# Expert stages of a macaron transformer block: answers copied out a quarter step sooner, last sends unpaced, and the second gated stage's end rearranged

## The reference

```python
x = L0_attn_x
x = x + 0.5 * _L0_ffn_ref(_layernorm(x), expert_sel, keys, values)        # 32 gated experts, top 4
x = x + _L0_attn_ref(_layernorm(x), Wq, ..., projection)                  # linear attention, 16 heads
x = x + 0.5 * _L0_ffn_ref(_layernorm(x), expert_sel, keys, values)        # the second gated stage
x = x + 0.5 * _L1_ffn_ref(_layernorm(x), Wg, W1, b1, W2, b2)              # experts, first time
x = x + _L1_attn_ref(_layernorm(x), P_q, P_k, P_v, P_o)                   # softmax diagonal, 16 heads
x = x + 0.5 * _L1_ffn_ref(_layernorm(x), Wg, W1, b1, W2, b2)              # experts, second time

def _L1_ffn_ref(x, Wg, W1, b1, W2, b2):    # 8 experts, 2 of them for each token
    gates = softmax(xt @ Wg); idx1, idx2 = best and second best expert of each token
    pos1, pos2 = position of the token among its expert's tokens, in order of choice
    xe[idx, pos] += xt * keep
    h = gelu(xe @ W1 + b1);  ye = h @ W2 + b2
    out = ye[idx1, pos1] * w1 + ye[idx2, pos2] * w2
```

## Time and profile before

| what | value |
|---|---|
| median of 3 runs | 1787.54 us (1783.36 to 1790.53) |
| the profiled execution | 1795.37 us, its span 1793.6 us |
| PE busy | 1441.7 us, 80% of the span |
| DVE busy | 1343.0 us, 75% |
| ACT busy | 1077.9 us, 60% |
| POOL busy | 858.8 us, 48% |
| granted PE clock, mean | 0.925 of full speed |

### The profile page before, as it was taken

How to read it: one execution, slowest core, us unless ns; L and a number is a source line. 1 busy time by engine, 2 the same in 40 slices (tenths; PEclk the granted TensorE clock), 3 DMA queues, 4 the chain that set the end, 5 groups by cost and what they waited for, 6 DMA issues and landing times. The chain is left out here.

```text
span 1793.6 us, 30589 instructions
## 1 busy us (share of the span) xinstructions
PE 1441.7 (80%) x8651; PEld 1048.8 (58%) x8653; DVE 1343.0 (75%) x3826; ACT 1077.9 (60%) x2260; POOL 858.8 (48%) x742
## 2 busy tenths in 40 slices
PE   5899988896999994998527888888888699679880
PEld 4677767654666653776415666566566466357660
DVE  7588887565667666776676999999999667757766
ACT  6677752364122325777437999999999522267770
POOL 6666642210034343565626666666666124636663
PEclk9899998898999996999859999999999899789995
DMA  5997001000001114222129930000000001122225
GB/s 106 142 176 115 1 1 25 1 1 24 16 30 43 30 33 93 55 67 60 41 85 183 179 59 1 1 1 1 1 1 1 1 16 34 42 59 59 59 57 143
DMA packets 182175, 91.71 MB, mean 51 GB/s; under 512 B 43829, under 2 KB 176902, under 8 KB 182048
## 3 DMA queue, kind: packets, MB, share of 16 engines
q1 hardware_dynamic: 167840, 71.19, 21.5%
q0 software_dynamic: 9984, 16.89, 2.9%
q10 hardware_dynamic: 4224, 2.10, 0.4%
HBM read 32.59 MB, written 61.18 MB: 52 GB/s over the span
## 5 line engine op out<-in xcount | busy, mean ns | idle before, releaser
L2523 DVE CUSTOM_DVE_ANT_0 psum<-psum,cmask 128x128 f32<-128x128 f32 (+7 forms) x512 | 375.5, 786 | 28.5 <-PE psum L2433 28.1
L2494 ACT ACTIVATE psum<-psum,gate 128x128 f32<-128x128 f32 (+7 forms) x512 | 367.0, 719 | 41.2 <-DVE gate L2523 33.8
L2180 POOL DMA_INDIRECT answers<-ed,answer_to x184 | 198.0, 1076 | 71.7 <-issue 45.4
L1258 PE MATMUL psum<-raw_all,w 128*128 128x512 f32 x384 | 195.4, 592 | 3.1 <-DVE raw_all L1383 1.5
L628 PE MATMUL psum<-xl,wreg 128*128 128x512 f32 x320 | 182.8, 571 | 11.2 <-PEq L89 10.9
L1173 POOL TENSOR_TENSOR hl<-hg,hh 128x512 fp32r<-128x512 f32 x96 | 124.4, 1296 | 83.1 <-ACT hh L1089 80.3
L1381 DVE SCALAR_TENSOR_TENSOR raw_all<-psum,hg 128x512 f32<-128x512 f32 x128 | 88.1, 691 | 70.3 <-PE psum L630 67.2
L174 POOL TENSOR_TENSOR spare_p<-spare_p 128x1 f32<-128x1 f32 x62 | 21.3, 344 | 226.3 <-DVE row_no L750 109.4
L629 PE MATMUL psum<-xh,wreg 128*128 128x512 f32 x320 | 127.3, 398 | 0.0
L630 PE MATMUL psum<-xh,wreg 128*128 128x512 f32 x320 | 127.0, 397 | 0.0
L2433 PE MATMUL psum<-spare_sets_room 64*128 64x384 f32 (+3 forms) x768 | 93.1, 375 | 41.9 <-ACT psum L2494 41.9
(11 more groups left out here) (410 smaller groups left out, 4046.1 us busy)
## 6 DMA issues: line engine op xcount, KB each, us to landing
rows<-blank SPq DMA_DIRECT2D x146, 258.0 KB, 7.1
row<-rows SPq DMA_DIRECT2D x46, 256.0 KB
raw_all<-answers SPq DMA_DIRECT2D x32, 256.0 KB, 3.4
w<-in_L_ffn_W_dram SPq DMA_DIRECT2D x16, 256.0 KB
answers<-ed,answer_to POOLq DMA_INDIRECT x184
x<-in_L_attn_x_dram SPq DMA_DIRECT2D x4, 512.0 KB, 5.7
out_dram<-x ACTq DMA_DIRECT2D x8, 256.0 KB
rawD<-in_L_ffn_values_dram SPq DMA_DIRECT2D x4, 256.0 KB, 7.0
```

The costliest lines, as they stand in the source:

```text
L1258: pe.matmul(bank(B_OUT[i % 2]), col(dn, j), hidden[:, n % HID, :], start=(j == 0), stop=(j == nf - 1)).then_inc(S["dn_done"], 1)
L2180: pool.indirect_dma_start(answers, bass.IndirectOffsetOnAxis(ap=answer_to[:, out.odd, t:t + 1], axis=0), y_row[:, out.odd, t, :], None, bo ...
L2494: return act.activation(src, src, ACT.Exp, bias=kept_at(arg, u, q, a), scale=-1.0, accum_out=kept_at(esum, u, q, a))
L2523: return dve.tensor_tensor_reduce(src, src, mask, 1.0, 3e38, ALU.add, ALU.min, kept_at(arg, u, q, a))
```

## The change

In `sorted_ffn`, for the second gated stage alone: ACT rounds the expert weights at step 7 of each period instead of step 10. POOL makes the first expert's remainders ahead of the loop over the blocks and in the loop those of the next expert, so that the eighth pair of products stands ahead of the sends of block 6 and no longer ahead of those of block 7. DVE leaves `heads_low` out and goes from the scaled logits straight to the positions. POOL runs one more `apart` behind its last sends, which brings `spaced` to 9.

In `moe_experts`, in both expert stages: in the opening iteration DVE copies the first expert's up weights before it waits for the first rows, and in the first of the two stages it then waits for `spaced` at 9 and runs `heads_low` there. In every iteration `leave` stands at j = 1, right behind the remainder of that step, instead of at j = 2. The sends of blocks 20 and 21 have no pacing waits (before, only block 22 had none).

```diff
--- before.py
+++ after.py
@@ -942,7 +942,7 @@
             act.activation(o_dn[:, k * BLK:(k + 1) * BLK], bank(B_O[k]), ACT.Copy)
 
 
-    MOE_AT = 10
+    MOE_AT = 7
     staged = w32[:, 3, :].rearrange("p (a w n) -> p a w n", a=2, w=2)
 
     def moe_sems():
@@ -1425,18 +1425,21 @@
             experts(dve, S)
             dve.wait_ge(S["step"], NORMS * NB)
             dve.tensor_tensor(L, L, kept_rs[:].unsqueeze(2).to_broadcast([P, NT, E1]), ALU.mult).then_inc(S["logits_scaled"], 1)
-            if first:
-                heads_low(dve, H)
             positions(dve, S)
 
         def gpsimd(pool):
             def paced(k, m):
                 return min(nf * (k + 1) + PLACE + 2 + m * nf // 8, NB * nf)
 
+            if first:
+                moe_low(pool, M, 0)
             for k in range(NB):
-                if first:
-                    moe_low(pool, M, k)
+                if first and k + 1 < E1:
+                    moe_low(pool, M, k + 1)
                 send_rows(pool, k, S, paced)
+            if first:
+                pool.wait_ge(S["spaced"], NB)
+                apart(pool, spare_p).then_inc(S["spaced"], 1)
 
         def sync(sp):
             if first:
@@ -1444,6 +1447,7 @@
                 sp.wait_ge(S["dn_done"], NB * nf)
                 heads_load(sp, H, S)
 
+        S["heads"] = H
         return Stage(S, tensor, scalar, vector, gpsimd, sync)
 
 
@@ -1941,7 +1945,7 @@
         B_UP, B_OUT, B_BACK, B_XT = (0, 1, 2, 3), (4, 7), 5, 6
 
 
-        UP_AT, DOWN_AT, LEAVE_AT = (0, 0), (1, 1), 2
+        UP_AT, DOWN_AT = (0, 0), (1, 1)
 
         class Block:
 
@@ -2142,20 +2146,27 @@
                 e_last, e_now, e_next = (
                     dve.value_load(expert_of[0:1, bass.ds(k.n + 1, 1)], min_val=0, max_val=E1 - 1) if k.there() else None
                     for k in (last, b, nxt))
+                opening = not b.loop and b.c == -1
+                if opening:
+                    up_weights(nxt, e_next, 0)
+                    up_weights(nxt, e_next, 1)
+                    if before["heads"]:
+                        dve.wait_ge(before["spaced"], NB + 1)
+                        heads_low(dve, before["heads"])
                 for j in range(Q):
                     if j == 0 and last.there():
                         low(last, Q - 1)
                     if j >= 1 and b.there():
                         low(b, j - 1)
+                    if j == 1 and out.there():
+                        leave(out)
                     if j == 0 and nxt.there():
                         next_low(nxt)
                     for k in range(2):
-                        if j == UP_AT[k] and nxt.there():
+                        if j == UP_AT[k] and nxt.there() and not opening:
                             up_weights(nxt, e_next, k)
                         if j == DOWN_AT[k] and b.there():
                             down_weights(b, e_now, k)
-                    if j == LEAVE_AT and out.there():
-                        leave(out)
                     if j == 3 and last.there():
                         answer_bias(last, e_last)
 
@@ -2175,13 +2186,13 @@
                         pool.wait_ge(S["spaced"], out.n)
                     apart(pool, spare_p).then_inc(S["spaced"], 1)
                     for t in range(BT):
-                        if t and out.n + 2 <= SPARSE:
+                        if t and out.n + 4 <= SPARSE:
                             pool.wait_ge(S[("b2_set", "oT_ready", "back_done")[t - 1]], out.n + 2)
                         pool.indirect_dma_start(answers, bass.IndirectOffsetOnAxis(ap=answer_to[:, out.odd, t:t + 1], axis=0),
                                                 y_row[:, out.odd, t, :], None, bounds_check=2 * T - 1, oob_is_err=False
                                                 ).then_inc(y_sent[out.odd], 16)
 
-            pool.wait_ge(before["spaced"], NB)
+            pool.wait_ge(before["spaced"], NB + (before["heads"] is not None))
             for c in range(SPARSE + 2):
                 one(Block(0, c, False))
```

## The result

The changed kernel took 1772.01 us (median of 4 runs, 1768.44 to 1774.31), the kernel before, beside it, 1786.49 us (4 runs): 14.5 us less, ratio 0.9916 [0.9887, 0.9945].

The account below looks back on a forecast made before the run. No engine was full; PE paced the expert stages, with rows or sends ending last at openings and ends. 4.6 + 3 + 2.6 - 0.3 = 9.9 us gave 1777.6 us against 1787.54, range 1772.5 to 1786.

Parts of the forecast that it names:

- (a): End of the second gated stage: PE's first turn of rows comes sooner, gain 4.6 us, bounds 2.5 and 5.
- the tiny product: DVE's small product behind the last block's norm, second gated stage: 3.19 us before, forecast at 0.2 us.
- the group: POOL's eight sends at the second gated stage's end: 12.36 us before, forecast at 10.8 us.
- Cover: First expert stage's opening: `heads_low` ends at 698.8, 0.4 us before `next_low` could start behind PE's first turn.
- (b): Inside the expert stages: earlier `leave` shortens PE's holes for rows, gain 3 us, ceiling 12, floor -2.
- (c): Ends of both expert stages: POOL's last sends end sooner, 1.3 us each, together 2.6 us, bounds 0 and 1.5 each.
- The ceiling of 12 us: Inside the expert stages: most the earlier `leave` could gain, 9 holes for rows at 1.37 us each.
- (d): Opening of the second expert stage: up-weight casts fall on POOL's last row sends, cost 0.3 us, bounds 0 and 0.5.
- The rows' way gains nothing: Rival, expert stages: pacing waits and ACT end last in nearly every hole; 6.9 us gained, 1780.6; chance 0.28.
- POOL becomes the pace: Rival, expert stages: sends falling on casts make POOL slower than PE's block, 11 us lost, 1791.6; chance 0.08.

Follow-up runs that it names:

- before_again: The kernel before, unaltered, run once more for a trace: 1792.14 us (1 run).
- after_third: The changed kernel, unaltered, run again as the measure for others: 1770.21 us, 0.9895 of the kernel before.
- send_late: The changed kernel with POOL's first send of each block held until the second remainder of the block after next: 1786.65 us, 0.9981 of the kernel before.
- unpaced_all: The changed kernel without any wait that spaces the four sends of a block: 1795.51 us, 1.0035 of the kernel before.
- gated_only: The changed kernel with `leave` back at j = 2 and the old pacing rule, so the gated stage's edits alone: 1759.6 us, 0.9978 of the kernel before.
- leave_only: The kernel before with `leave` alone moved to j = 1, ahead of the casts: 1757.53 us, 0.9970 of the kernel before.

## Why the prediction was right and where it failed

- **(a) was right where it was priced, and wrong in a term put at nothing.** Forecast 4.6 us, measured 4.61 in the record pair: the tiny product at 0.16 us, the group at 10.75. Cover forecast 0.4 us, 0.17 left. In the quicker kind the same distance is 4.7 us shorter (30.6 to 25.9). But of the pair of remainders moved forward and ScalarE's roundings three steps up it says "I cost both at nothing", since GpSimd has nothing to send there. It looked at GpSimd alone: VectorE is at its choice, its products took 0.83 and 1.19 us instead of 0.20 and 0.19, PE waited 1.60 us, and the stage is 1.7 us longer. That is the clash of 3.19 us over again, in another place. What is left, 2.9 us, fits the 3.5 and 2.3 us that the gated part brings in time.
- **(b) is the step that failed**: "in about half the holes ACT is late too and the hole would only change its name, so I take 3 us". The sum priced the waits for rows alone, as a shift of so much per hole. In the record pair those shrank by 6.8 us, and PE's other waits, put at nothing, by 6.5; the stages are 14.3 us shorter. That pair flatters the change: by the medians 14.5 us less 2.9 for (a) and 1.1 for (c) leave some 10.5. In the slower kind the moved copy alone brings 15.6 us in time, and the single traces of before_again and after_third have 351.6 and 332.2 us of stages; in the quicker kind it brings 5.6. The holes in the slower kind are not shifted rows: with every wait for rows taken away, nothing was gained. They are one or two blocks over 10 us and several of about 8 in a stage, with waits for ScalarE and for rows in them and a clock that falls behind them. How the sends lie decides whether they open, as send_late (all back) and unpaced_all (25 us worse) show; how a send holds ScalarE up is not shown. The ceiling of 12 us, nine holes of 1.37, had no room for it.
- **The clock has no term in the prediction.** It priced each hole at its own length, though the windows of the kernel before show 0.98 and, past the opening, 0.96 in the stages. In the record pair that is 1.0 us of the 14.3; between the two kinds it is some 7 us.
- **(c) was mis-sized**: 2.6 forecast, 1.1 measured. In the first stage the forecast let the group of block 20 follow on a send that ended 5.46 us before PE's last turn (873.46 and 878.92). In the changed kernel the group ahead ended 4.81 us before it (863.09 and 867.90): it had waited 1.17 us for the answer bias. The earlier copy was there, GpSimd was not. In the second stage the group of block 19 did start 1.36 us sooner against PE's last turn, as forecast, but took 6.7 us instead of 6.2, and the three behind it 16.4 instead of 16.2.
- **(d)** cost nothing, 0.3 had been taken.
- **The rivals.** "The rows' way gains nothing" was right in its reason for the slower kind (others end last in the holes) and wrong in its consequence. "POOL becomes the pace" fell: sends beside casts do take up to 1.47 us, but the kernel got faster all the same, with groups of 6.0 to 6.3 us at the median. That a pacing wait holds up an earlier send had been counted as a loss; unpaced_all shows for the slower kind that the pacing earns far more than it costs.
- **Luck.** In the quicker kind the copy alone brings 5.6 us in time, the very sum of (b) and (c), 3 + 2.6. By the traces of gated_only and leave_only it is two errors against each other: 4.5 us in the stages, and 0.5 at their ends (from PE's last turn to the last send's end, 12.5 and 12.0 us in gated_only, 12.0 and 12.0 in leave_only).

## What to carry to other kernels

Where a stage is a loop over blocks and its pace is uneven, list the lengths of the blocks first: a shift of some tenths in every hole and a few blocks of nearly twice the length need different terms, and the second kind can hang on a transfer that is not on the chain. Taking away the wait named in the profile tests its price in one run; if the hole changes its name, look for what else is late in the same block. Before a gap at the head of a loop is put down to the jump, ask the view of the source line for the sequencer's own work there: here it was three register loads. When work moves out of a clash, look at what every engine does in its new place, and not only at the engine that does it. Give a hole on TensorE a second term for the clock when the granted clock of the stage is under 1.

## What the hardware showed that was not expected

- The kernel before takes 1763 us in three groups and 1790 in two, and the changed one 1755 and 1770: one change is worth half a per cent in one kind of group and one per cent in the other (0.9952 and 0.9895, intervals apart), and one chip number stands under both kinds.
- Loading three expert numbers from SBUF into registers kept VectorE's sequencer busy for 1.8 to 2.0 us at the head of each block, 0.30 us for each load and up to 0.19 for the register operation behind it.
- In the slower kind, with GpSimd's four sends in one row, ScalarE had its longest stop (4.73 us) and the kernel took 1795.5 us; with the same sends spread over the block by waits it had one of 0.48 us in that stage, and the kernel took 1770.2.
- With the products of two SBUF operands gone from beside the sends, the group went from 12.36 to 10.75 us, against the rule of the Trainium skill weighed in the prediction ("SBUF — State Buffer", who interferes with whom). Of the three only the third, which reads its operands in strides (L932), lay beside the long send of 2.59 us, and in before_again beside the two of 1.96 and 1.46; in the kernel before, the sends beside the first two took 0.97 and 1.16.
